# Dequantization moved between the steps of the first FFN tile, and the FFN tiles regrouped from four pairs to 1-2-2-2-1

## The reference, cut to what matters

```python
q, k, v = X @ Wq.T + bq, X @ Wk.T + bk, X @ Wv.T + bv       # X: 16 x 2048 x 1024
attn = softmax(where(j > i, -inf, q @ k.T / 32), axis=-2)
x = layernorm(X + attn @ v)
h = x
for blk in range(3):                                        # weights 2*blk and 2*blk + 1
    y = qlora(h, w[2*blk])                                  # y1
    y = gelu(layernorm(y) * gamma + beta)
    h = qlora(y, w[2*blk + 1]) + h                          # y2
out = layernorm(x + h)
# qlora: x @ ((q/7.5 - 1) * scale).T + bias + (x @ la.T) @ lb.T, all weights 1024 x 1024
```

## Time and profile before

| What | us |
|---|---|
| Median of two runs (2774.11 to 2774.5) | 2774.3 |
| The profiled execution | 2769.95 |
| Its span, first to last instruction of the slowest core | 2768.4 |
| TensorE busy with matmuls | 1630.0 (59%) |
| VectorE busy | 1037.8 (37%) |
| ScalarE busy | 988.4 (36%) |

### The profile page before, as it was taken

How to read it: one execution, slowest core, us unless ns; L and a number is a source line. 1 busy time by engine, 2 the same in 40 slices (tenths; PEclk the granted TensorE clock), 3 DMA queues, 4 the chain that set the end, 5 groups by cost and what they waited for, 6 DMA issues and landing times.

```text
span 2768.4 us, 21874 instructions; the slowest of 8 cores (2753.0 to 2768.4 us)
## 1 busy us (share of the span) xinstructions
PE 1630.0 (59%) x6880; PEld 680.6 (25%) x6880; DVE 1037.8 (37%) x1049; ACT 988.4 (36%) x1472; POOL 56.8 (2%) x100
## 2 busy tenths in 40 slices
PE   0899891099989011114558545775467656665953
PEld 0344340044433000001223222332123222222321
DVE  1113536211343534342532633255414526152262
ACT  0331203032111212223464446445454454445444
POOL 0000000000000000010000000000000000000000
PEclk9999996599999555557789858988678887678975
DMA  5220022521012356665110050100240000501001
GB/s 169 77 69 16 31 92 109 186 82 55 16 46 77 125 195 231 226 214 185 49 43 31 0 182 31 61 31 0 67 146 31 31 31 1 182 31 61 31 1 61
DMA packets 72543, 228.63 MB, mean 83 GB/s; under 512 B 6768, under 2 KB 7024, under 8 KB 66032
## 3 DMA queue, kind: packets, MB, share of 16 engines
q1 hardware_dynamic: 61680, 181.09, 20.3%
q0 software_dynamic: 10752, 46.14, 4.2%
HBM read 181.07 MB, written 46.14 MB: 82 GB/s over the span
## 4 chain that ended last, share of the span: by engine, by line
PE 47%; ACT 16%; DVE 12%; DMA 12%; issue 7%; PEld 2%; DVEq 1%; SPq 1%; PEldq 1%; ACTq 0%; POOL 0%; POOLq 0%
PE ps L747 23%; PE ps L258 8%; DMA PL<-sc_t 5%; PE ps L370 5%; PE ps L313 4%; ACT PL L923 2%; PE ps L727 2%; DMA PL<-wq_t 2%; PEld ps L446 2%; DMA PL<-xt 2%; PE ps L975 2%; DVE PL L915 2%; DVE PL L913 2%; PE ps L729 2%; DMA PL<-weffs 1%
## 5 line engine op out<-in xcount | busy, mean ns | idle before, releaser
L747 PE MATMUL ps<-PL 128*128 128x512 bf16 x3072 | 724.0, 392 | 333.2 <-ACT PL L923 308.7
L747 PEld LDWEIGHTS ps<-PL 128*128 128x128 bf16 x3072 | 305.8, 100 | 726.1 <-issue 388.7
L258 PE MATMUL ps<-PL 128*128 128x512 bf16 x1024 | 226.2, 384 | 212.2 <-DVE PL L211 209.0
L891 DVE TENSOR_TENSOR e2s<-e2s,m2s 128x512 f32<-128x512 f32 x32 | 22.1, 691 | 551.1 <-ACT e2s L883 551.1
L616 PE MATMUL ps<-PL 32*128 32x512 bf16 x48 | 28.1, 585 | 302.1 <-DVEq L639 182.2
L258 PEld LDWEIGHTS ps<-PL 128*128 128x128 bf16 x1024 | 100.6, 99 | 337.4 <-issue 220.6
L770 ACT ACTIVATE PL<-ps,fb 128x512 bf16<-128x512 f32 x192 | 132.0, 687 | 140.9 <-PE ps L729 140.6
L783 DVE SCALAR_TENSOR_TENSOR PL<-ps,fb,PL 128x512 f32<-128x512 f32 x192 | 144.2, 751 | 93.7 <-PE ps L747 93.3
L975 PE MATMUL ps<-eye,PL 128*128 128x128 f32 x256 | 90.6, 438 | 142.6 <-ACT PL L989 77.2
L446 PE MATMUL ps<-PL 128*128 128x512 bf16 x640 | 141.7, 385 | 20.2 <-ACTq L171 20.2
L370 PE MATMUL ps<-PL 128*128 128x512 bf16 x640 | 139.4, 379 | 7.0 <-issue 4.3
(11 more groups left out here) (74 smaller groups left out, 1608.5 us busy)
## 6 DMA issues: line engine op xcount, KB each, us to landing
PL<-weffs SPq DMA_DIRECT2D x24, 2048.0 KB, 9.3
PL<-xt SPq DMA_DIRECT2D x32, 1024.0 KB, 5.7
PL<-qw_t SPq DMA_DIRECT2D x48, 512.0 KB, 4.7
PL<-sc_t SPq DMA_DIRECT2D x48, 512.0 KB, 6.2
x1s<-PL POOLq DMA_DIRECT2D x16, 1024.0 KB, 4.2
PL<-x1s SPq DMA_DIRECT2D x64, 256.0 KB, 7.5
out<-PL POOLq DMA_DIRECT2D x32, 512.0 KB, 4.3
weffs<-PL POOLq DMA_DIRECT2D x48, 256.0 KB, 6.2
```

The lines of the kernel that those rows point to most:

```text
L258: last = e.matmul(ps[bank][:], bfv(area + c * 512, 1024)[:, s * 128:(s + 1) * 128], xtbf[:, c * 2048 + tc * 512:c * 2048 + (tc + 1) * 512] ...
L747: last = e.matmul(ps[bank][:], bfv(WSL[sl], 8192)[:, c * 1024 + s * 128:c * 1024 + (s + 1) * 128], src_mv[:, c * 512:(c + 1) * 512], start ...
```

## The change

- The body of the dequantization loop becomes a function `dequant_w(w)`. Its LoRA matmuls use banks 6 and 7 for every chunk, so chunk c waits for VectorE's end of chunk c-1.
- The loop over four pairs becomes a function `emit_group` over a list of tiles, called for (0), (1, 2), (3, 4), (5, 6) and (7). A tile's slot is still its number modulo 2.
- In the first group a hook writes `dequant_w` into the program in front of the weight loads: weights 0 and 1 at the head of the group; weight 2 behind the gelu of block 0 and weight 3 behind its y2; weight 4 and 5 likewise in block 1.
- At the head of every group SP issues the x loads of all its tiles first and then the weights 0 and 1.
- The waits for the end of dequantization go to tile 1, the first to use slot 1; banks 4 and 5 no longer wait for it. They are counts of the end of group 0.

```diff
-        for w in range(6):
+        def dequant_w(w):
...
                 for c in range(EC):
-                    bank = 4 + 2 * (c % 2)
-                    if c >= 2:
-                        wt(e, "ve", dq_ve[c - 2])
-                    e.matmul(ps[bank][:], bfv(O_LAR, 1024)[0:32, c * 128:(c + 1) * 128],
+                    if c >= 1:
+                        wt(e, "ve", dq_ve[c - 1])
+                    e.matmul(ps[6][:], bfv(O_LAR, 1024)[0:32, c * 128:(c + 1) * 128],
...
-        for pair in range(NTILE // 2):
...
-            xmA = x1_load(tA, exA)
-            wl = {0: w_load(0), 1: w_load(1)}
-            xmB = x1_load(tB, exB)
...
+        def emit_group(gname, ts, ex_x1=None, ex_cast=None, hook=None):
...
+            for j in (0, 1):
+                if hook:
+                    hook(j)
+            for t in ts:
+                xm[t] = x1_load(t, (ex_x1 or {}).get(t, ()))
+            wl[0] = w_load(0)
+            wl[1] = w_load(1)
...
                 if w1 + 2 < 6:
+                    if hook:
+                        hook(w1 + 2)
                     wl[w1 + 2] = w_load(w1 + 2)
...
                 if w2 + 2 < 6:
+                    if hook:
+                        hook(w2 + 2)
                     wl[w2 + 2] = w_load(w2 + 2)
...
+        def dq_hook(j):
+            for w in range(j + 1):
+                if w not in _dq_emitted:
+                    _dq_emitted.add(w)
+                    dequant_w(w)
+
+        emit_group("ffng0", (0,),
+                   ex_x1={0: (("sp", attn_end["sp"]), ("ve", attn_end["ve"]))},
+                   hook=dq_hook)
...
+        emit_group("ffng1", (1, 2), ex_x1=ex1, ex_cast=exc1)
+        emit_group("ffng2", (3, 4))
+        emit_group("ffng3", (5, 6))
+        emit_group("ffng4", (7,))
```

More of the change, by code:

```diff
@@ L554, in build_program @@
         attn_end = dict(cnt)
-        scope("dequant")
         w_sw_marks = []
-        prev_lac = cnt["ve"]
-        for w in range(6):
+        _dqst = {"prev_lac": cnt["ve"]}
+        def dequant_w(w):
+            prev_lac = _dqst["prev_lac"]
             la_ld = cnt["gl"]
@@ L612, in _ @@
                 for c in range(EC):
-                    bank = 4 + 2 * (c % 2)
-                    if c >= 2:
-                        wt(e, "ve", dq_ve[c - 2])
-                    e.matmul(ps[bank][:], bfv(O_LAR, 1024)[0:32, c * 128:(c + 1) * 128],
+                    if c >= 1:
+                        wt(e, "ve", dq_ve[c - 1])
+                    e.matmul(ps[6][:], bfv(O_LAR, 1024)[0:32, c * 128:(c + 1) * 128],
                              bfv(O_LBR, 1024)[0:32, 0:512], start=True, stop=True)
-                    last = e.matmul(ps[bank + 1][:], bfv(O_LAR, 1024)[0:32, c * 128:(c + 1) * 128],
+                    last = e.matmul(ps[7][:], bfv(O_LAR, 1024)[0:32, c * 128:(c + 1) * 128],
                              bfv(O_LBR, 1024)[0:32, 512:1024], start=True, stop=True)
@@ L624, in _ @@
                 for c in range(EC):
-                    bank = 4 + 2 * (c % 2)
+                    bank = 6
                     wt(e, "se", se_bq + c + 1)
@@ L1005, in build_program @@
         fbcols = [fb[:, w * 8:(w + 1) * 8] for w in range(6)]
-        for pair in range(NTILE // 2):
[L1007 to L1012, removed]
-            xmA = x1_load(tA, exA)
-            wl = {0: w_load(0), 1: w_load(1)}
-            xmB = x1_load(tB, exB)
-            cm = {tA: cast_in(tA, IBASE[0], xmA),
-                  tB: cast_in(tB, IBASE[1], xmB, extra=exBc)}
+        def emit_group(gname, ts, ex_x1=None, ex_cast=None, hook=None):
+            nonlocal_osb = None
+            scope(gname)
+            xm = {}
+            wl = {}
+            cm = {}
+            for j in (0, 1):
[5 more added lines that the diff above has]
+            wl[1] = w_load(1)
+            for t in ts:
+                cm[t] = cast_in(t, IBASE[t % 2], xm[t],
+                                extra=(ex_cast or {}).get(t, ()))
             for blki in range(3):
@@ L1020, in build_program @@
                 gel = {}
-                for t in (tA, tB):
+                for t in ts:
                     y_mms(t, w1, wl[w1], cm[t], "y1", fbcols[w1])
-                fin = {t: ln_fin2(t) for t in (tA, tB)}
-                for t in (tA, tB):
+                fin = {t: ln_fin2(t) for t in ts}
+                for t in ts:
                     gel[t] = apply_gelu(t, blki, fin[t])
                 if w1 + 2 < 6:
+                    if hook:
+                        hook(w1 + 2)
                     wl[w1 + 2] = w_load(w1 + 2)
-                for t in (tA, tB):
+                for t in ts:
                     in1 = IBASE[t % 2] if blki == 0 else IBASE[t % 2] + 8192
```

27 lines of the change are left out of this document (16 added, 11 removed).

## The result

The changed kernel takes 2904.6 us in the median against 2774.3: a ratio of 1.0471, 95% interval 1.0459 to 1.0483, so 4.7% slower. The forecast was 2899 us, slower. The profiled execution took 2904.61 us with a span of 2903.1, which is 134.7 over the span before; by the ratio of the runs the change costs 130.7 us. In some executions of either kernel the cores of one die run longer at a lower granted clock; the ratios are taken from the executions without this.

What follows compares the result with a forecast made beforehand. Dequantization was taken as bound by its loads, the FFN by waits between dependent steps. Lone tiles less cover some 55, boundaries 67.5 and banks 3 made 125.2 over 2768.4, so 2899 us in the median, 4.5% slower; range 2865 to 2938.

Steps and rivals of the forecast that it cites:

- D1: Group 0: dequantization of weight 1, ending at 1069.3; D2 to D5 are those of weights 2 to 5, 47.3 us each.
- The two turns: Group 0, from D2 to D3 and D4 to D5: 17.3 us each, LoRA loads standing behind a weight load.
- Lone tiles: Groups of one tile: gaps lack a partner's matmuls; last tile 233.0 us, 44.5 dearer than half a pair.
- The cover: Group 0: the part of tile 0 overlapped with dequantizations; the prediction's steps imply 22.3 us.
- the 21.0 of the second y1: Lone last tile: the y1 matmuls of its second block take 21.0 us, against 22.7 from an idle start.
- the 15.3 for transposes and copies: Tail of a lone tile: 32 transposes with copies take 15.3 us, within a tail of 39.4.
- Boundaries: Group starts: weights wait behind x loads; net 19.0 us at two boundaries, 29.5 from group 0 to 1, 67.5 in all.
- the 2.0: Boundaries: taken off the 21.0 us wait, for ScalarE's wait for A's last store and weights no longer sharing with it.
- Banks: Dequantization with one bank pair: LoRA matmuls wait until the chunk before is drained; 3 us in all, between 0 and 53.
- Cheap loads: Rival at boundaries and turns: nothing waits behind what was issued ahead, 29 us saved, 2870 us; chance 0.12.
- Bank pair: Rival in dequantization: every chunk pays 1.1 us, 53 instead of 3, 2949 us; chance 0.09.
- Hidden: Rival in group 0: D2 to D5 run back to back with tile 0 beneath, 2783 us, no change; chance 0.06.

Runs made afterwards that it cites:

- weights first: Changed kernel with both weight loads ahead of all x loads at the head of each group: 2860.6 and 2864.7 us in two executions.
- the two other kernels with this order: New load order with lone tiles and all six dequantizations at the head of group 0, ratio 1.0573; new load order alone in the kernel before, ratio 1.0216.
- the run: Kernel before, with the LoRA matmuls of every chunk in banks 6 and 7 and nothing else changed: 2774.25 us, ratio 1.0003.
- three finer orders: Changed kernel with weights 2 to 5 dequantized chunk by chunk within tile 0 (1.0459), in clumps of two to four (1.0531), clumps with casts ahead (1.0522).

## Why the prediction was right

**The shape.** Stages came in the order forecast, with the turns serial. Measured from the end of D1 (at 1074.5 on this core, 5.2 late from its attention part), y1 of tile 0 starts after 13.0 us (forecast 13.6), D2 ends after 99.7 (100.2), D3 after 162.8 (164.8), D4 after 244.6 (247.4), D5 after 308.3 (312.0), and group 1 starts after 439.4 (437.6). The two turns were 15.8 and 16.1 us, not 17.3, in another make-up than forecast: the last write landed in 2.3 us, with no load beside it, and the LoRA load took 10.10 (1178.43 to 1188.53) behind the weight, so that it landed only 1.2 us behind the adds of y2.

**Lone tiles: mechanism right, size too small.** The steps imply 221.1 + 233.0 - 377.0 = 77.1 us for two tiles alone; the kernel with only these and the bank pair shows 92.8. The cover was too small as well, 22.3 where 26.8 were measured, and offsets a part. In the changed kernel the last tile took 240.3 instead of 233.0. One half of the 7.3 comes from the matmuls. TensorE's timeline of the last tile:

```profile
2707.95 16.47 PE L744 MATMUL ps<-PL 128*128 128x512 bf16 x64 [22.57 <-ACT PL L920]
2726.43 5.30 PE L744 MATMUL ps<-PL 128*128 128x512 bf16 x16 [2.01 <-DVE PL L786]
...
2788.81 3.61 PE L744 MATMUL ps<-PL 128*128 128x512 bf16 x16 [1.85 <-DVE PL L786]
```

The first y2 with its last adds took 18.5 us instead of 17.0, and the second y1 with its gap 45.1 instead of 43.5. Two terms were too small on this core. In the first y2 not eight but some twelve matmuls go at the lower of the clock's two levels, 1.2 GHz (granted clock 0.50 to 2711.5, 0.78 from there to 2715.0), so the 64 take 16.47 us and not 15.5. And the 21.0 of the second y1 fails: behind a wait of 2.01 us the first eight matmuls go at 0.42 each again (3.37 us, the last row of the chain; granted clock 0.54), as behind a long wait. Behind 1.85 us before the third, 16 matmuls take 3.61 us at 2.4 GHz (granted clock 1.00).

The length of the wait alone does not divide the two. The last tile with weights first:

```profile
2683.46 3.61 PE L744 MATMUL ps<-PL 128*128 128x512 bf16 x16 [2.01 <-DVE PL L786]
```

Here, and on cores 2, 3 and 5 of the changed kernel's own execution, the same 2.01 us were followed by the upper level. Over all cores of the changed kernel and of the seven others with lone tiles, TensorE fell back six times behind a wait of 2.0 us at such a place, always when the y2 ahead had taken 16.5 to 16.8 us for its 64 matmuls; where that had taken 15.3 to 15.8 us it never did. That is a coincidence seen, not a cause shown: what decides is left open.

The other half is the tail. Of the timeline, the statistics of the last tile and the first copy's table:

```profile
2850.03 0.76 DVE L843 CAST sqd<-PL 128x512 bf16<-128x512 f32 x2
...
2858.43 0.38 PE L859 MATMUL ps<-sqd,ones_b 128*128 128x512 bf16 x1
...
2875.21 1.28 ACT L986 ACT_TABLE_LOAD   x1 [9.94 <-PE ps L972]
```

Statistics of one tile take 8.8 us (2850.03 to 2858.81), not half of the 13.6 of two: with no partner, VectorE and ScalarE, which feed TensorE, wait for the buffer that it frees (VectorE 2.14 us behind its first two casts). I halved a row of a pair where a lone tile does not get half. And a table load of 1.28 us stands bare in front of the first copy. That is no matter of the partner, since a pair has it too (2740.55): the 15.3 for transposes and copies were read behind it and left it out.

**Boundaries: the net right, by two errors that cancel in part.** Net 19.0 were taken for groups 1 and 2. They are 14.3 and 13.4 longer than group 3, which itself took 2.9 more than a pair before; against the kernel with the order undone they are 18.3 and 19.6, and the new order alone cost 18.2 to 20.0 per pair in the kernel before. So 13.4 to 20.0 by the yardstick, with the forecast near the top. But the wait itself was taken as 21.0 and took 17.66 and 17.41 (18.4 to 22.3 at the like boundaries of the two other kernels with this order), and the 2.0 taken off for ScalarE's shorter wait did not come: its table load ahead of the second tile's copies waits 8.00 and 7.83 us for the last store, against 8.03 and 8.45 before. The first boundary was 29.8 (29.5 forecast). SP and VectorE at the start of group 2:

```profile
1884.32 4.93 SPq L688 DMA_DIRECT2D PL<-x1s  x8
...
1896.66 2.29 DVE L702 CAST PL<-PL 128x4096 bf16<-128x4096 f32 x1 [23.20 <-DMA PL<-x1s]
```

The weight, issued at 1889.45, landed 12.10 us later, 4.9 us behind x. In these last 5 us (1896.6 to 1901.6) the DMA engines moved 392 GB/s, about 2 MB, which is the size of the weight. So it moved behind x and not beside it. The Trainium skill (DMA: Bandwidth & Descriptors, Queues, rings and completion order) has each DMA engine take a ring's descriptors in their order, and this trace agrees. That the order costs time at all is shown by the kernels with it changed, +60 and -42.

**Banks.** 3 us were set; the run shows 0.8 with an interval of 3 to either side (1.0003 [0.9992, 1.0014]). The Trainium skill (Perfetto Trace Analysis, Matmuls) would have independent groups of matmuls rotate through the banks; here, where each chunk waits for its loads, giving that up has no price that the runs can tell from nothing.

**The sum** from the terms above: +5.2 from the start of group 0's chain, +1.8 up to group 1, -1.8 and -2.8 for two groups, +2.9 for the third, +7.3 for the last tile: 12.5 before rounding, which is 2903.1 less the 2890.6 forecast ahead of the banks. The errors have both signs, so that the forecast lies only 5.6 us from the median is partly luck, and so is the net of a boundary.

**The rivals.** Cheap loads (2870): no, the first boundary waits 29.8 us and not 19.3, and the later ones 17.4 and more and not 14.3; only the turns, 15.8 and 16.1 against 14.6, came near it. Bank pair (2949): no, 1.0003. Hidden (2783): no, and three finer orders do not hide it either.

## What to carry to other kernels

The worth of working on two tiles at a time lies in the waits between dependent steps that one fills for the other; a tile alone pays them in full (here 93 us for two of eight tiles), and the small covers at the edges too. Writing a piece of work between two steps of another is no overlap where engines run their queues in order: ask for every engine what stands behind what, how many buffers are ahead, and what each change of function costs. In a load queue, what the next step waits for goes ahead of what cannot be issued yet; and where both cannot be had, the wait only moves (weights first gained at group 1 and lost at tile 0). Two tiles staggered by half a block, with the last block written for its own case, used the gaps that the change paid for (2705.5 us).

## What the hardware showed that was not expected

- A wait of TensorE of 2.01 us was followed by eight matmuls at the lower clock level (3.37 us), one of 1.85 us was not; on other cores and in another kernel 2.01 us were not either.
- A load of 128 KB issued right behind a 2 MB load took 10.10 and 10.62 us to land.
- A 256 KB store with no load beside it landed in 2.3 us, where the median of the 48 is 6.2.
- ScalarE's table loads, 1.28 us each, cost more than the conversions of 1.06 us as soon as these alternate with other functions.
